# Layer norm statistics staged by ScalarE and GpSimd in pairs of tiles, instead of by VectorE

## The chip, the cores and the metric

The kernel runs on all 8 cores of one Trainium2 chip, one sequence of the batch on each core, with no traffic between them. The metric is the device time in microseconds of the slowest core. A core has five engines with a queue each: TensorE (PE, matmuls), VectorE (DVE), ScalarE (ACT), GpSimd (POOL) and SyncE (SP), which only issues DMAs here. ScalarE and GpSimd issue some of the DMAs too.

## The reference

Two layers on x of shape 8 x 2048 x 1024, in float32. LN is the layer norm without weights.

```python
def _layernorm(x, axis=-1, eps=1e-5):
    m = jnp.mean(x, axis=axis, keepdims=True)
    v = jnp.var(x, axis=axis, keepdims=True)
    return (x - m) / jnp.sqrt(v + eps)

x = x + L0_attn(_layernorm(x))   # minGRU-like scan h; layer norm of h, times gamma, + beta, + its input
x = x + L0_ffn(_layernorm(x))    # 1024 -> 4096 -> 1024, weights fake-quantised to 8 bits, plus LoRA
x = x + L1_attn(_layernorm(x))   # time-mix, k, v, r products, wkv scan, output product
x = x + L1_ffn(_layernorm(x))    # three products of 1024 x 1024, tanh
```

So there are five layer norms: of x before each of the four blocks, and of the scan's result h inside the first. The fake quantisation needs the largest absolute value of each of the two weight matrices.

## The kernel before

**Layout.** Each core holds its sequence transposed: 1024 features are 8 row blocks (`kk` or `m`, 0 to 7) of 128 partitions, and 2048 steps of time are 4 tiles (`n`, 0 to 3) of 512. `X0` and `H0` are 8 blocks of 128x2048 float32 each, `XB0` the same in bf16, `E0` four blocks (`EX[0]` and `EX[1]` hold the rows of a norm), `SC` scratch with the slots `SCR[0]` to `SCR[4]` of 128x512 float32. The eight PSUM banks are `PB0` to `PB7`.

**Queues and waits.** The order of the work on each engine is the order of the source. The helper `body` (line 105) opens a block of instructions for one engine; it waits first for what `k.dep` has gathered and for the engine's own last count, then runs the given function. `mark` counts up the engine's semaphore, `chain` does so and waits for it.

**Statistics of a norm.** The features lie along partitions, so the sums over them are made on TensorE: a 128x128 matrix of ones (`ONESB`) times the tile gives the sum in every partition. `ln_stats` (line 284) goes over the 32 tiles of a tensor in SBUF, `kk` outside and `n` inside. Each tile is staged into one of two slots (`SCR[0]` and `SCR[1]`, each seen as 1024 bf16): the first half takes a bf16 copy, the second the square. Then two matmuls add them into banks `n` and `NT + n` over the eight `kk`. A slot may be filled again when its matmuls are done (`slot_tok`). With `stage="v"`, the default and what all three callers use, VectorE does the copy and the square of one tile in a block. The function also has a branch `stage == "sg"`, which no caller uses before the change.

`_ln_rows` (line 347) then has VectorE scale the sums, form the variance and its reciprocal, and ScalarE take the square root. It is unchanged, as is `ln_stream_stats` (line 379), which does the statistics of the third and fourth norm on tiles loaded from DRAM; the fourth (line 1345) has a `stage="sg"` of its own, with one tile at a time.

**The three callers.** (1) Line 475, norm of x: `X0` is loaded by two DMAs of 4 MB, followed by the small parameters; the weights `WZ` and `WH` are loaded by GpSimd's queue. ScalarE first makes small exponentials of the parameters (`p0s`, `p0d2`). After the rows, VectorE and GpSimd make the normalised `XB0`. (2) Line 683, norm of h. The loop before it (m over 8 blocks, n over 4 tiles) has products on TensorE, sigmoids on ScalarE, combinations and a scan per m on VectorE (`scan_done[m]`). Between them VectorE takes the absolute maximum of the weights, in chunks loaded through `qring` (`Pass1`, line 521). `pass1_fin` (line 645) stands between loop and norm: a GpSimd reduction over the partitions, a memset on VectorE, a broadcast matmul on TensorE (`bcm`) and four small VectorE operations. After the norm h, scaled and added to its inputs, makes `H0` (`comb_done`). (3) Line 759, norm of `H0`. Before it stand a second `pass1_fin` and eight DMAs on ScalarE's queue that spill `H0` to DRAM (`spl`, line 754), the one of block m when `comb_done` of that block is there.

**`Pass1`.** It keeps the token of its last reduction in `self.prev`, None at first, on which the next reduction waits.

Of the kernel before, what the change touches and what calls it, by code (L numbers as in the profile page):

```python
# [181 lines left out]
def build(T=2048, debug=False):  # L182
# [54 lines left out]
    EX = [E0[:, i * RT:i * RT + T] for i in range(4)]  # L237
# [5 lines left out]
    with nc.Block() as blk:  # L243
        k = K(nc, blk)
# [226 lines left out]
        def ln1_tok(kk, n):  # L471
# [1 line left out]

        k.dep(["tensor"], at=tmax(smalls_v))
        ln1_rows = ln_stats(lambda kk, n: Xr[kk][:, n * NSZ:(n + 1) * NSZ],
                            ln1_tok, EX[0], EX[1])
        stats_T = ("tensor", k.snap("tensor"))

        xhat_tok = {}
# [41 lines left out]
        class Pass1:  # L521

            def __init__(self, hbm, nrows, ping, gate=None):
                self.hbm = hbm
                self.ping = ping
                self.chunks = [(kk, c) for kk in range(nrows)
                               for c in range(hbm.shape[1] // QCH)]
                self.ci = 0
                self.prev = None
                def mz(v, ping=ping):  # L530
                    v.memset(MX[:, ping:ping + 1], 0.0)
                    v.mark()
                k.V(mz)

            def emit(self, n):
                end = min(self.ci + n, len(self.chunks))
                while self.ci < end:
                    ci = self.ci
                    kk, c = self.chunks[ci]
                    ping = self.ping  # L540
                    slot, tok = qring.load(
                        ci, self.hbm[kk * 128:(kk + 1) * 128,
                                     c * QCH:(c + 1) * QCH])
                    k.dep(["vector"], at=tmax(tok, self.prev))
                    def red(v, ci=ci, slot=slot, ping=ping):
                        v.tensor_reduce(MX[:, 12:13], slot, AX.X,
                                        OP.max, apply_absolute_value=True)
                        v.chain()
                        v.tensor_max(
                            MX[:, ping + (ci + 1) % 2:ping + 1 + (ci + 1) % 2],  # L550
                            MX[:, ping + ci % 2:ping + 1 + ci % 2],
                            MX[:, 12:13])
                        qring.release(ci, ("vector", v.mark()))
                    k.V(red)
                    self.prev = ("vector", k.snap("vector"))
                    self.ci += 1
# [18 lines left out]
        scan_done = {}  # L575
# [69 lines left out]
        def pass1_fin(fcol, qcol, bank, vtok):  # L645
# [19 lines left out]
            def qsc(v, qcol=qcol, bank=bank):  # L665
# [15 lines left out]
        qfc_tok = pass1_fin(f_fc, 0, 7, f_fc_tok)  # L681

        lnh_rows = ln_stats(lambda kk, n: HD[kk][:, n * NSZ:(n + 1) * NSZ],
                            lambda kk, n: scan_done[kk], EX[0], EX[1])

        xring = Ring(k, [EXf[2][:, i * 512:(i + 1) * 512] for i in range(4)],
                     ["rr0", "rr1", "rr2", "rr3"], issue_eng="sync",
# [1 line left out]
        comb_done = {}  # L689
# [62 lines left out]
        for m in range(8):  # L752
            k.dep(["scalar"], at=comb_m[m])
            def spl(y, m=m):
# [2 lines left out]
            sp2_at[m] = ("sp2w%d" % m, 16)  # L757

        ln2_rows = ln_stats(lambda kk, n: Hr[kk][:, n * NSZ:(n + 1) * NSZ],
                            lambda kk, n: comb_done[(kk, n)], EX[0], EX[1])  # L760
        xh2_tok = {}
        k.dep(["vector", "gpsimd"], at=tmax(ln2_rows))
        def xh2_v(v):
# [778 lines left out]
```

How the kernel before makes its waits and increments, by code:

```python
    def mark(self):  # L47
        K = self._K
        c = K.ch[self._n]
        assert self.last is not None, "mark with no pending instruction"
        self.last.then_inc(c.sem, 1)
        c.val += 1
        self.last = None
        return c.val
# [1 line left out]
    def chain(self):  # L56
        v = self.mark()
        self._e.wait_ge(self._K.ch[self._n].sem, v)
# [1 line left out]
    def wait(self, name, val):  # L60
        if val > 0:
            self._e.wait_ge(self._K.ch[name].sem, val)
# [1 line left out]
    def dma(self, name, out, in_, **kw):  # L64
        K = self._K
        c = K.ch[name]
        ins = self._e.dma_start(out=out, in_=in_, **kw)
        ins.then_inc(c.sem, 16)
        c.val += 16
        self.last = None
        return c.val
# [34 lines left out]
        def run(eng):  # L106
            ctx = Eng(self, eng, name)
            pend = self.pend[name]
            own = self.ch[name]
            if own.val > pend.get(name, 0):
                pend[name] = own.val
            if pend:
                for p, v in sorted(pend.items()):
                    if v > 0:
                        eng.wait_ge(self.ch[p].sem, v)
                pend.clear()
            fn(ctx)
            if ctx.last is not None:
                ctx.mark()
# [149 lines left out]
            def f(g):  # L269
                ins = g.dma_start(out=out, in_=in_, **kw)
                ins.then_inc(c.sem, 16)
                g.last = None
# [1209 lines left out]
        def fin(y):  # L1482
            for name, v in sorted(fin_vals.items()):
                if v > 0:
                    y.wait_ge(k.ch[name].sem, v)
```

## Time and profile before

| | us |
|---|---|
| median of 2 runs | 2946.62 (2943.77 to 2949.47) |
| the profiled execution | 2951.28 |
| its span on the slowest core (core 3) | 2949.7 |
| spans of the 8 cores | 2912.0 to 2949.7 |
| VectorE busy | 1456.2 (49%) |
| TensorE busy, matmuls | 1334.9 (45%) |
| ScalarE busy, of it table loads | 654.4, 309.2 |
| GpSimd busy | 276.1 (9%) |

Busy times are sums over one core's span; an engine may be nearly idle overall and still set the pace of a stage. All times below are from core 3, in microseconds from the start of its span. ACT_TABLE_LOAD is an instruction by which ScalarE loads the tables of its functions; nobody writes it in the source, the compiler places it.

### The profile page before, as it was taken

To read this page: it belongs to the slowest core of one execution; us is meant where nothing else is said; L and a number is where in the kernel's file an instruction comes from. 1 tells how busy PE (TensorE), PEld (TensorE's weight loads), DVE (VectorE), ACT (ScalarE), POOL (GpSimd) and SP (SyncE) were. 2 spreads that over 40 slices of the span, in tenths; PEclk is the share of its full clock that TensorE was granted. 3 is DMA by queue.
4 is the path that set the end of the run, shared out by engine and by line. 5 is a ranking of instruction groups with operands and counts; after the bars stand their busy time and mean duration, and the time that the engine had idled before them with its cause. 6 is when DMAs were issued, how large, how long until landed. Compare 5 with 4: busy or idle time off the path is not lost.

```text
span 2949.7 us, 18381 instructions; the slowest of 8 cores (2912.0 to 2949.7 us)
## 1 busy us (share of the span) xinstructions
PE 1334.9 (45%) x4868; PEld 483.7 (16%) x4868; DVE 1456.2 (49%) x1702; ACT 654.4 (22%) x766; POOL 276.1 (9%) x219
## 2 busy tenths in 40 slices
PE   3144443004044804878888330265055454130986
PEld 0011110000000300333333100122022111000332
DVE  3866667888898996101010136654945411034232
ACT  0023330000287400030313000045034300250003
POOL 0300000230310001000000002400300000222000
PEclk9997776555555955989999755677577767555998
DMA  7223331340033330101010661100100144823006
GB/s 186 86 85 108 107 111 32 78 121 15 17 108 108 101 106 13 43 15 56 2 58 1 120 152 38 43 0 0 38 5 1 22 94 87 153 86 114 1 7 207
DMA packets 73843, 200.95 MB, mean 68 GB/s; under 512 B 9440, under 2 KB 9440, under 8 KB 70928
## 3 DMA queue, kind: packets, MB, share of 16 engines
q1 hardware_dynamic: 59952, 165.76, 19.6%
q0 software_dynamic: 11776, 19.34, 4.5%
q10 hardware_dynamic: 2016, 14.68, 1.3%
q8 instruction: 44, 0.72, 0.1%
q14 instruction: 55, 0.45, 0.1%
HBM read 179.24 MB, written 39.85 MB: 74 GB/s over the span
## 4 chain that ended last, share of the span: by engine, by line
DVE 38%; PE 22%; DMA 18%; ACT 11%; issue 7%; POOL 1%; DVEq 1%; SPq 1%; ACTq 0%; POOLq 0%
PE PB L38 22%; DVE SC L38 10%; DVE X L38 10%; DMA SC<-SP 8%; DVE E L38 7%; ACT L38 5%; DVE AT L38 4%; DVE H L38 3%; DVE XB L38 3%; ACT SC L38 3%; DMA E<-SP 2%; ACT X L38 2%; DMA E<-WPRT 2%; DVE MX L38 2%; DMA AT<-SP 2%
## 5 line engine op out<-in xcount | busy, mean ns | idle before, releaser
L38 ACT ACT_TABLE_LOAD x241 | 309.2, 1283 | 2280.9 <-PE PB L38 974.6
L38 PE MATMUL PB<-XB,X 128*128 128x512 bf16 x1280 | 294.1, 390 | 154.6 <-POOL XB L38 97.5
L38 PE MATMUL PB<-XB,H 128*128 128x512 bf16 x896 | 233.1, 420 | 270.5 <-DVE X L38 162.0
L38 PE MATMUL PB<-E,H 128*128 128x512 bf16 x1152 | 274.5, 403 | 68.8 <-DVE X L38 50.1
L38 PE MATMUL PB<-X,H 128*128 128x512 bf16 x512 | 148.4, 461 | 323.4 <-ACT SC L38 114.9
L38 PE MATMUL PB<-SC,ONESB 128*128 128x512 bf16 x320 | 154.8, 584 | 267.0 <-DVE SC L38 154.9
L38 DVE TENSOR_SCALAR AT<-PB,QS,SMT 128x512 f32<-128x512 f32 x32 | 25.9, 810 | 465.1 <-PE PB L38 337.7
L38 PEld LDWEIGHTS PB<-XB,X 128*128 128x128 bf16 x1280 | 125.1, 100 | 324.0 <-issue 188.9
L38 PEld LDWEIGHTS PB<-XB,H 128*128 128x128 bf16 x896 | 91.0, 106 | 413.1 <-issue 338.1
L38 PEld LDWEIGHTS PB<-E,H 128*128 128x128 bf16 x1152 | 117.3, 103 | 225.9 <-issue 107.0
L38 PE MATMUL PB<-H,X 128*128 128x512 bf16 x512 | 120.8, 397 | 21.1 <-ACT X L38 7.9
L38 PEld LDWEIGHTS PB<-X,H 128*128 128x128 bf16 x512 | 57.4, 114 | 414.8 <-issue 378.5
L38 PE MATMUL PB<-E,ASL 16*128 16x512 bf16 x64 | 37.1, 580 | 174.6 <-ACT E L38 93.7
L38 DVE TENSOR_TENSOR X<-PB,SC 128x512 f32<-128x512 f32 x32 | 22.1, 691 | 182.0 <-DMA SC<-SP 182.0
L38 PE MATMUL PB<-MX,SC 1*128 1x1 f32 x4 | 1.1, 343 | 198.6 <-DVE SC L38 198.6
L38 PE MATMUL PB<-SC,ASL 16*128 16x512 bf16 x64 | 36.5, 570 | 119.9 <-DVE H L38 90.6
L38 ACT ACTIVATE E<-PB,SMT,QS 128x512 bf16<-128x512 f32 x128 | 89.1, 776 | 0.4
L38 DVE CAST H<-PB 128x512 bf16<-128x512 f32 x64 | 39.7, 682 | 98.6 <-PE PB L38 98.6
L38 POOL TENSOR_TENSOR E<-E 128x1024 f32<-128x1024 f32 x28 | 78.1, 2789 | 95.9 <-DMA E<-SP 92.4
L38 PEld LDWEIGHTS PB<-SC,ONESB 128*128 128x128 bf16 x320 | 21.7, 103 | 397.2 <-issue 397.2
L38 DVE TENSOR_SCALAR SC<-E,DRV 128x1024 f32<-128x1024 f32 x16 | 12.1, 753 | 127.0 <-ACT SC L38 127.0
L38 DVE TENSOR_SCALAR E<-PB 128x512 f32<-128x512 f32 x40 | 24.4, 680 | 91.6 <-PE PB L38 91.6
(136 smaller groups left out, 1927.1 us busy)
## 6 DMA issues: line engine op xcount, KB each, us to landing
AT<-WFCT SPq DMA_DIRECT2D x32, 512.0 KB, 3.7
E<-WFCT SPq DMA_DIRECT2D x32, 512.0 KB, 3.9
SC<-WPRT SPq DMA_DIRECT2D x32, 512.0 KB, 3.7
SC<-SP SPq DMA_DIRECT2D x64, 256.0 KB, 3.5
AT<-SP SPq DMA_DIRECT2D x32, 512.0 KB, 3.7
E<-SP SPq DMA_DIRECT2D x32, 512.0 KB, 3.7
E<-SP SPq DMA_DIRECT2D x56, 256.0 KB, 5.1
X<-XT SPq DMA_DIRECT2D x2, 4096.0 KB, 28.9
```

Of the source, the lines that this page charges most:

```text
L38: ins = f(*args, **kw)
```

## The change

`ln_stats` is called with `stage="sg"` in all three places. In that branch the tiles go in pairs. ScalarE makes the two bf16 copies (an activation with the function Copy), GpSimd the two squares (a product of the tile with itself), each in a block of its own. Both blocks wait for the matmuls of both slots and for the tokens of both tiles; TensorE then waits for both engines and does the four matmuls of the pair in one block. The slots and their number, the sums and their order stay.

In `Pass1` the token `self.prev` is set, after the memset that clears the running maximum, to VectorE's count at that point.

```diff
         ln1_rows = ln_stats(lambda kk, n: Xr[kk][:, n * NSZ:(n + 1) * NSZ],
-                            ln1_tok, EX[0], EX[1])
+                            ln1_tok, EX[0], EX[1], stage="sg")
...
                 k.V(mz)
+                self.prev = ("vector", k.snap("vector"))
...
         lnh_rows = ln_stats(lambda kk, n: HD[kk][:, n * NSZ:(n + 1) * NSZ],
-                            lambda kk, n: scan_done[kk], EX[0], EX[1])
+                            lambda kk, n: scan_done[kk], EX[0], EX[1],
+                            stage="sg")
...
         ln2_rows = ln_stats(lambda kk, n: Hr[kk][:, n * NSZ:(n + 1) * NSZ],
-                            lambda kk, n: comb_done[(kk, n)], EX[0], EX[1])
+                            lambda kk, n: comb_done[(kk, n)], EX[0], EX[1],
+                            stage="sg")
```

## Rows read from the trace of the kernel before

**Rows 1.** The page: its header and the chain that ended last, by engine.
```profile
span 2949.7 us, 18381 instructions; the slowest of 8 cores (2912.0 to 2949.7 us)
...
DVE 38%; PE 22%; DMA 18%; ACT 11%; issue 7%; POOL 1%; DVEq 1%; SPq 1%; ACTq 0%; POOLq 0%
```

**Rows 2.** Busy time by stretches: length, engines' busy us and counts, granted clock, DMA.
```profile
42.20:84.40 42.20, 32.38 (x64) 4.38 (x64) 32.91 (x65) 2.75 (x5) 0.00 (x0) 1.00 0.38 70
...
2555.00:2631.00 76.00, 32.38 (x64) 4.37 (x64) 0.00 (x0) 61.20 (x64) 33.22 (x32) 0.50 0.45 130
...
473.50:494.70 21.20, 15.18 (x30) 2.05 (x30) 16.42 (x33) 0.00 (x0) 0.00 (x0) 0.51 0.00 0
494.70:513.60 18.90, 10.06 (x34) 2.18 (x34) 16.43 (x33) 0.00 (x0) 0.00 (x0) 1.00 0.00 1
```

**Rows 3.** Timeline, first norm: start, duration, engine, operation, [idle before <-releaser].
```profile
42.20 0.43 DVE L38 CAST SC<-X 128x512 bf16<-128x512 f32 x1 [0.17 <-DVE DRV L38]
...
43.37 1.01 PE L38 MATMUL PB<-SC,ONESB 128*128 128x512 bf16 x2 [43.37 <-DVE SC L38]
...
44.93 0.21 ACT L38 ACTIVATE DRV<-DRV 128x8 f32<-128x8 f32 x1
...
45.90 0.43 DVE L38 CAST SC<-X 128x512 bf16<-128x512 f32 x1 [0.24 <-PE PB L38]
...
46.24 0.68 DVE L38 TENSOR_TENSOR SC<-X 128x512 bf16<-128x512 f32 x1
...
47.17 1.01 PE L38 MATMUL PB<-SC,ONESB 128*128 128x512 bf16 x2 [0.26 <-PE PB L38]
...
83.15 1.01 PE L38 MATMUL PB<-SC,ONESB 128*128 128x512 bf16 x2 [0.43 <-DVE SC L38]
```

**Rows 4.** Timeline, statistics of the fourth norm.
```profile
2555.62 1.03 POOL L38 TENSOR_TENSOR SC<-AT 128x512 bf16<-128x512 f32 x1 [8.58 <-DMA AT<-SP]
...
2557.92 1.01 PE L38 MATMUL PB<-SC,ONESB 128*128 128x512 bf16 x2 [51.04 <-POOL SC L38]
...
2559.08 1.04 POOL L38 TENSOR_TENSOR SC<-E 128x512 bf16<-128x512 f32 x1 [1.19 <-PE PB L38]
...
2566.66 1.28 ACT L38 ACT_TABLE_LOAD   x1 [3.09 <-DMA AT<-SP]
...
2567.95 0.63 ACT L38 ACTIVATE SC<-AT 128x512 bf16<-128x512 f32 x1
...
2568.83 1.01 PE L38 MATMUL PB<-SC,ONESB 128*128 128x512 bf16 x2 [3.79 <-ACT SC L38]
```

**Rows 5.** Groups of instructions from 2555 to 2631: count | busy, mean ns | idle before.
```profile
L38 ACT ACT_TABLE_LOAD x32 | 41.1, 1283 | 228.7 <-DMA AT<-SP 224.1 <-DMA E<-SP 2.2
```

**Rows 6.** Timeline, ScalarE in the loop after the first norm.
```profile
176.03 0.69 ACT L38 ACTIVATE X<-PB,DRV 128x512 f32<-128x512 f32 x1
176.62 1.26 ACT L38 ACTIVATE E<-PB,SMT 128x512 f32<-128x512 f32 x2
```

**Rows 7.** All instructions on the ones matrix: ns min/median/max, first and last start.
```profile
L38 PE MATMUL PB<-SC,ONESB x320: 376/586/634, 43.4 to 2630.3; 128*128 128x512 bf16 x160
```

**Rows 8.** Timeline: first scan, end of the loop, broadcast, last statistics pair of LNH.
```profile
192.50 4.42 DVE L38 TENSOR_TENSOR_SCAN H<-X 128x2048 f32<-128x2048 f32 x1
...
453.47 1.26 ACT L38 ACTIVATE E<-PB,SMT 128x512 f32<-128x512 f32 x2
...
471.76 0.55 PE L38 MATMUL PB<-MX,SC 1*128 1x1 f32 x2 [42.66 <-DVE SC L38]
...
512.82 0.59 PE L38 MATMUL PB<-SC,ONESB 128*128 128x512 bf16 x2 [0.54 <-DVE SC L38]
```

**Rows 9.** Timeline: last spill of H, last statistics pair of the second norm.
```profile
668.85 0.33 ACTq L67 DMA_DIRECT2D SP<-H  x1
...
712.51 1.01 PE L38 MATMUL PB<-SC,ONESB 128*128 128x512 bf16 x2 [0.26 <-PE PB L38]
```

**Rows 10.** Groups of GpSimd's instructions over the span, shapes kept apart.
```profile
L38 POOL TENSOR_TENSOR XB<-SC,E 128x512 bf16<-128x512 f32 x16 | 24.4, 1524 | 2.3
```

## The prediction

> **What bounds the kernel now.** I read the header and the chain of work that ended last on the page first. The chain goes by VectorE for 38% of the span and by TensorE for 22% [rows 1]: no single engine is full, the kernel is a row of stages that wait for one another. So the three stages that the change touches have to be found in the trace and read one by one. They are the three places where the ones matrix is multiplied with a staged tile: 43 to 84 us (first norm, "LN1"), 474 to 513 us (norm of the scan's result, "LNH") and 671 to 714 us (second norm, "LN2").
>
> In each of them VectorE stages a tile (a cast and a square), TensorE multiplies it, and nothing else runs: in LN1 the stretch holds 32.9 us of VectorE and 32.4 us of TensorE, with ScalarE and GpSimd almost empty [rows 2]. The timeline shows the tempo. VectorE starts a cast at 45.90 and its square ends at 46.92 (46.24 + 0.68); the matmul pair starts 0.25 later, at 47.17, takes 1.01, and the next cast into that slot follows 0.24 behind it. One slot's circle is 1.02 + 0.25 + 1.01 + 0.24 = 2.52 us, and there are two slots, so a tile costs 1.26 us [rows 3]. From the first pair at 43.37 to the last at 83.15 are 31 tiles: 1.28 us each. In all three stages the normalised values wait for the last matmul, so what a stage grows by goes straight to the end of the kernel. No work stands behind the statistics on VectorE that could be drawn forward: the next thing in its queue is the rows, which read the finished sums.
>
> **The change, part by part.** All three calls take the branch "sg", which no stage of this program takes through `ln_stats` now. It removes 32 casts and 32 squares per stage from VectorE and puts the casts on ScalarE and the squares on GpSimd. It also moves from tiles to pairs of tiles: both engines wait until both slots are free, fill both, and TensorE then makes four matmuls. With two slots and pairs of two, the slots are no longer filled while the others are multiplied. So the circle of a pair must be added up end to end. The nearest work is the last norm (LN4, 2555 to 2631 us), which already stages with ScalarE and GpSimd, though from a loaded tile and with one tile at a time.
>
> 1. *Release of the slot.* TensorE's pair ends at 2558.93 (2557.92 + 1.01), GpSimd starts at 2559.08: 0.15 us. I take it for ScalarE too [rows 4].
> 2. *ScalarE.* Each block of instructions of LN4 begins with a table load: 32 loads in 32 blocks, 1283 ns each [rows 5], and the load comes after the wait, not beneath it: at 2566.66 it starts when the DMA is there, and the copy follows at 2567.95, 1.29 later [rows 4]. The copy takes 0.63. Here a block has two copies with no wait between them. In the loop after LN1 two such activations of 0.69 start 0.59 apart (176.03 and 176.62), so they overlap by 0.10 [rows 6]; two copies thus take 0.53 + 0.63 = 1.16. ScalarE: 1.29 + 1.16 = 2.45.
> 3. *GpSimd, in parallel.* A square takes 1.03 to 1.04 [rows 4]. Two take 2.08 if they touch; a gap as wide as 0.20 between them would make it 2.28. Either is under ScalarE's 2.45, so I cost GpSimd at nothing: the table load covers it, by 0.17 to 0.37 us.
> 4. *Hand-over to TensorE.* The copy ends at 2568.58, the matmul starts at 2568.83: 0.25 [rows 4].
> 5. *Four matmuls.* A pair takes 1.01 and a single one has a median of 0.586 [rows 3, 7], so each further one adds 0.42: 1.01 + 0.85 = 1.86.
>
> The circle: 0.15 + 2.45 + 0.25 + 1.86 = 4.71 us per pair, against 2.52 for two tiles now. The new one is nearly twice as long, because casts and squares, though parallel now, have got the table load in front and the matmuls behind them.
>
> Then each stage's start and end, with 15 circles after the first pair (15 x 4.71 = 70.7):
> - LN1. ScalarE still has the small exponentials to do and is free at 45.14 (44.93 + 0.21), where VectorE began at 42.20 [rows 3]. Table load and copies from 45.21 end at 47.66, matmuls 47.91 to 49.77, last ones end at 120.4. Now they end at 84.16: **+36.3**.
> - LNH. ScalarE's last evacuation before it ends at 454.7 [rows 8], so the first pair lies ready. TensorE must first take the broadcast of the maximum, which waits for VectorE's memset behind its last reductions and ends at 472.31 (471.76 + 0.55) [rows 8]. First four matmuls to 474.3, last to 544.9, against 513.41: **+31.5**.
> - LN2. ScalarE's queue holds the eight spills of H first; the last one is issued at 668.85 and done at 669.18 [rows 9]. So load and copies run to 671.7, matmuls to 673.8, the last to 744.5, against 713.52: **+30.9**.
>
> Sum: +98.7 us. What VectorE is spared (35 us per stage) is worth nothing, as it only waits for the same sums.
>
> The granted clock of TensorE: LNH began at 0.51 and rose to 1.00 near 494.7 us, and there the pair fell from 1.01 to 0.59 us; TensorE had been busy 15.2 of the 21.2 us before [rows 2]. LN2 and LN4 never show the fast pairs. LN4 has TensorE busy 32.4 of 76 us at 0.50 (the level of 1.2 GHz), and the new stages would have 1.86 of 4.71, much the same share. So I count every matmul slow, LNH's second half too, whose loss is in the +31.5.
>
> The other edit sets `self.prev` to VectorE's own count after the memset. `body` waits for the engine's own last count in any case, and that count is never lower; the instructions stay the same. Cost nothing; there is nothing that it could hide.
>
> A rule of the Trainium skill speaks against step 2. "ScalarE: Activation LUTs", section "Table sets: the hidden batching unit", has copy in every set as filler, and says that functions of one set need one load between them; by it the pairs would need no loads and the circle would be GpSimd's. This case's trace does not agree for this program: 32 loads for 32 blocks of copies alone. Against step 3 stands "GPSIMD Engine Reference", section "Elementwise — side-by-side cycle accounting", with a two-input operation about twice as long as on VectorE. That would be an estimate of 1.37 us for a square, and +13 us or so in the sum; the trace has 1.04.
>
> **The rivals.**
> - *GpSimd sets the circle.* The 16 products of GpSimd after LN1 take 1.52 us each [rows 10], with VectorE at work beside most of them. If the squares take that long, GpSimd needs 3.04, 0.59 over ScalarE's 2.45: 45 x 0.59 = +27 more, 3072 us. For it: no square from X or H was ever made by GpSimd. Against it: LN4's squares are the same operation and shape with VectorE idle, as it will be here.
> - *No table load in the circle* (absent or beneath the wait). GpSimd then leads with 2.08: 45 x 0.37 = 17 less, and 1.3 each off LN1 and LN2: 3026 us. Against it are all 32 loads of LN4 [rows 5]. By the skill's rule on table sets the time would come out here.
> - *TensorE at the fast level.* The four matmuls then take 1.01 (0.59 for the first two, and 2 x 0.21, as the shortest single one is 0.376 [rows 7]): 48 x 0.85 = 41 less, 3004 us. LNH has shown the fast level; but after a stretch with a busy share nearly twice that of the new circle.
> - *The other side: the statistics run ahead.* They no longer need VectorE, and the scans' tiles come one by one, the first from 192.5 us [rows 8]. If ScalarE, GpSimd and TensorE took them as they come, only the last two pairs of LNH would be left, and it would be over at about 473 instead of 513.4 us; LN2 likewise, some 9 us after 669 instead of 45. Sum: 36 - 40 - 35 = -39 us, 2908 us, not slower. The point that decides is TensorE's queue: the broadcast of the maximum stands before the first statistics matmul and needs VectorE's last reduction (it starts at 471.76 [rows 8]), and at LN2 the spills stand before the copies. With only two slots nothing past the first pair can go ahead. Queues keep their order, so this falls.
>
> **How the numbers follow.** The profiled execution took 2951.28 us (span 2949.7); with 98.7 that is 3050.0. The median of the runs is 4.7 us lower, 2946.62, so the forecast is 3045.3 us, 3.3% slower. Chances: the forecast with its small errors 0.82; GpSimd sets the circle 0.08; no table load 0.04; TensorE fast 0.03; statistics ahead 0.02; something unseen 0.01. The range runs from the case without the load to that with GpSimd's slow squares, 3026 to 3072. That takes in the unknown widths too: no overlap of the copies is +4.5 us, GpSimd's gap nothing. All cases but the last two end over 2% slower (2946.6 x 1.02 = 3005.6; the case of the fast matmuls lies right at that line and I split it). Two per cent is about what a measurement of this kernel can tell from no change. Slower 0.95, within 2% 0.04, faster 0.01.
>
> **What would show it.** In the changed profile: in the three stages GpSimd squares and ScalarE copies of 128x512 from X and H, with a table load before each pair of copies, 48 more loads in all (289); matmuls of the ones matrix in fours of 1.86 us, whose starts lie 4.7 us apart; ScalarE's copy as what released TensorE; the rows on VectorE starting near 120.6 us instead of 84.3, then everything about 36 us late, 68 us after LNH and 99 us after LN2, and the same from there to the end. The step on GpSimd is wrong if TensorE waits for GpSimd in these stages; the step on the level if fours take 1.0 us; the step on the queues if the first fours of LNH come before 471 us. The whole forecast is wrong if one of the stages ends within 45 us, since then pairs overlap in a way I rule out, or if a later stage gives time back, for which I see no slack: what follows each norm waits for its rows.

## The result and the profile after

The changed kernel takes 3049.83 us (median of 11 runs), the kernel before 2947.43 us (10 runs beside it). The ratio is 1.0341, with a 95% interval of 1.0319 to 1.0364: 3.4% slower. The forecast was 3045.3 us, 3.3% slower. In some executions of any of these kernels the cores of one half of the chip show a lower clock and take some per cent longer; every ratio here is formed without them, and of the first measurement with four slots too few were left for a ratio.

The page of the changed kernel, header and busy times:

```profile
span 3040.3 us, 18446 instructions; the slowest of 8 cores (3016.0 to 3040.3 us)
...
PE 1334.9 (44%) x4868; PEld 491.3 (16%) x4868; DVE 1362.7 (45%) x1510; ACT 771.2 (25%) x910; POOL 371.7 (12%) x315
```

TensorE does the same work in the same busy time. VectorE has lost 93 us of work (1456.2 before), and the kernel is 102 us longer. What VectorE gave up has gone to ScalarE (+117 us) and GpSimd (+96 us), and more than half of ScalarE's share is table loads: 289 of them now, 241 before.

The timeline of the changed kernel at the start of the first norm, the counterpart of [rows 3] (start, duration, engine, operation, [idle before <-what ended it]):

```profile
46.96 1.28 ACT L38 ACT_TABLE_LOAD   x1
48.25 1.15 ACT L38 ACTIVATE SC<-X 128x512 bf16<-128x512 f32 x2
...
49.65 1.86 PE L38 MATMUL PB<-SC,ONESB 128*128 128x512 bf16 x4 [49.65 <-ACT SC L38]
...
51.65 1.28 ACT L38 ACT_TABLE_LOAD   x1 [2.25 <-PE PB L38]
51.72 2.04 POOL L38 TENSOR_TENSOR SC<-X 128x512 bf16<-128x512 f32 x2 [27.91 <-PE PB L38]
52.94 1.15 ACT L38 ACTIVATE SC<-X 128x512 bf16<-128x512 f32 x2
...
54.34 1.86 PE L38 MATMUL PB<-SC,ONESB 128*128 128x512 bf16 x4 [2.83 <-ACT SC L38]
...
120.36 1.86 PE L38 MATMUL PB<-SC,ONESB 128*128 128x512 bf16 x4 [2.83 <-ACT SC L38]
```

This is one turn of the circle, read from release to release. TensorE's four matmuls end at 51.51 (49.65 + 1.86). ScalarE's table load starts at 51.65 and its two copies end at 54.09. GpSimd starts at 51.72 and is done at 53.76. TensorE starts at 54.34, released by ScalarE ("ACT SC"), after 2.83 us of idleness. From the first four at 49.65 to the sixteenth at 120.36 are 15 turns: 4.71 us each. Nothing in this list overlaps but copy and square.

The stretches of the three norms in the changed kernel (length, then busy us and counts of TensorE, its weight loads, VectorE, ScalarE and GpSimd, the granted clock, DMA):

```profile
49.60:122.30 72.70, 29.83 (x64) 6.91 (x64) 0.00 (x0) 36.48 (x45) 30.52 (x30) 1.00 0.13 22
509.30:581.90 72.60, 29.83 (x64) 6.93 (x64) 0.49 (x4) 36.48 (x45) 30.52 (x30) 0.50 0.00 0
742.00:814.60 72.60, 29.83 (x64) 6.90 (x64) 0.00 (x0) 36.48 (x45) 30.52 (x30) 0.50 0.00 0
```

Three equal stretches of 72.6 us, where [rows 2] and the timeline of before had 38.5 to 41. VectorE does nothing at all in two of them. TensorE's 29.8, ScalarE's 36.5 and GpSimd's 30.5 us are each well under 72.6: no engine is full, their times add up.

Which core is the slowest differs from execution to execution, so I compared where the last statistics matmul ends on each of the 8 cores in the two profiled executions. These are means over the cores:

| end of | before | after | later by | forecast |
|---|---|---|---|---|
| first norm | 84.8 | 121.6 | 36.8 | 36.3 |
| norm of the scan | 512.9 | 579.0 | 66.1 | 67.8 |
| second norm | 713.2 | 811.5 | 98.4 | 98.7 |
| the span | 2930.2 | 3029.3 | 99.1 | 98.7 |

The loss arises in the three norms and nothing behind them gives any back. The slowest cores alone differ by 90.6 us (2949.7 and 3040.3): the cores of one execution lie up to 38 us apart, and most of that spread arises after the second norm, in both kernels.

### The profile page after: what moved, and what is told of

It is laid out like the page before. It is cut to its first block, busy times and chain, and to the rows that moved or that the text cites. A ratio compares the mean times of both kernels' runs of the same rounds, so it can differ in the third digit from the quotient of the medians.

```text
span 3040.3 us, 18446 instructions; the slowest of 8 cores (3016.0 to 3040.3 us)
## 1 busy us (share of the span) xinstructions
PE 1334.9 (44%) x4868; PEld 491.3 (16%) x4868; DVE 1362.7 (45%) x1510; ACT 771.2 (25%) x910; POOL 371.7 (12%) x315
## 4 chain that ended last, share of the span: by engine, by line
DVE 35%; PE 23%; DMA 17%; ACT 14%; issue 7%; POOL 1%; DVEq 1%; SPq 1%; ACTq 0%; POOLq 0%
PE PB L38 23%; DVE X L38 9%; DVE SC L38 8%; DMA SC<-SP 7%; DVE E L38 7%; ACT L38 6%; ACT SC L38 4%; DVE AT L38 4%; DVE H L38 3%; DVE XB L38 3%; DMA AT<-SP 3%; ACT X L38 2%; DMA E<-WPRT 2%; DVE MX L38 2%; DMA SMT<-SM 1%
## 5 line engine op out<-in xcount | busy, mean ns | idle before, releaser
L38 PE MATMUL PB<-E,H 128*128 128x512 bf16 x1152 | 278.4, 407 | 66.1 <-DVE X L38 47.6
L38 PEld LDWEIGHTS PB<-XB,H 128*128 128x128 bf16 x896 | 90.6, 105 | 409.1 <-issue 333.0
L38 PEld LDWEIGHTS PB<-SC,ONESB 128*128 128x128 bf16 x320 | 29.5, 117 | 480.1 <-issue 480.1
L38 PE MATMUL PB<-SC,ASL 16*128 16x512 bf16 x64 | 36.3, 566 | 119.7 <-DVE H L38 93.5
L38 DVE CAST H<-PB 128x512 bf16<-128x512 f32 x64 | 39.7, 682 | 98.4 <-PE PB L38 98.4
```

What stands on the lines that cost most here:

```text
L38: ins = f(*args, **kw)
```

## The experiments

Two ways to explain 4.71 us per pair were to be told apart. By the theory, the circle is long because filling and multiplying stand end to end, and the table load is one of the pieces on it. By its rivals, the load is the real cost, or GpSimd sets the pace, or ScalarE and GpSimd are just slow at the work. All edits are to the changed kernel unless something else is said. A pair's turn in the kernel before is 2.52 us.

**One norm alone.** The kernel before, with the new staging in the first norm only.

```diff
-                            ln1_tok, EX[0], EX[1])
+                            ln1_tok, EX[0], EX[1], stage="sg")
```

> The kernel before with stage="sg" in the first norm alone, and self.prev as before. Theory (each norm is a chain of its own that sets the end, so the costs add up): the first norm's last statistics matmul ends 36 us later and everything behind it shifts by that much, 2947 + 36 = 2983 us. Rival (a later stage gives time back, for instance through transfers that have landed by then, or the cost lies in one of the other two norms): less than 2970 us.

Measured: 1.0133 of the kernel before (1.0089 to 1.0177), which at 2947 us is +39 us (26 to 52), with 36 expected. The first norm's matmuls take 72.6 us here, as in the changed kernel, and on the mean over the cores they end 36.3 us later and the span 34.3 us later than in the kernel before (121.1 and 2964.5, against 84.8 and 2930.2). So the cost of a norm passes to the end nearly whole, and with the table above the three add up. In this execution the scan's norm took 41.1 us in VectorE's way on the slowest core, all with slow matmuls:

```profile
550.61 1.01 PE L38 MATMUL PB<-SC,ONESB 128*128 128x512 bf16 x2 [0.26 <-PE PB L38]
...
551.88 1.01 PE L38 MATMUL PB<-SC,ONESB 128*128 128x512 bf16 x2 [0.25 <-PE PB L38]
```

The fast second half that [rows 8] show for the kernel before, with pairs of 0.59 us, is thus no fixed part of it: here core 0 had it (37.4 us for the norm) and most others did not. In the profiled execution of the kernel before, the norm took 38.5 us on core 3, and 39.9 to 41.3 on the other cores.

**Four slots.** The slots `SCR[0]` to `SCR[3]`, so that a pair is filled while the one before is multiplied, with a wait before the first use of the two new ones (not shown here); nothing else.

```diff
-                    at = tmax(slot_tok[0], slot_tok[1],
+                    at = tmax(slot_tok[p0 % 4], slot_tok[(p0 + 1) % 4],
...
-                            sb = bc16(SCR[(p0 + j) % 2])
+                            sb = bc16(SCR[(p0 + j) % 4])
```

> The changed kernel with four staging slots (SCR 0 to 3) instead of two, so that a pair can be filled while the pair before it is multiplied. Theory (the cost is that filling and multiplying stand end to end): the pair's period falls from 4.71 us to ScalarE's own 1.29 + 1.15 + about 0.13 = 2.57 us, 45 x 2.14 = 96 us less, about 2954 us. Rival (ScalarE and GpSimd are slower at the work by themselves, whatever the slots): the period stays above 4 us and the time above 3020 us.

> The kernel with four slots once more, beside the one above: its period was 2.63 us, so 45 x 2.08 = 94 us less than 3050 are expected, 2956 us, some 0.4% over the kernel before and 15 us over four slots with one load.

Measured: 2961.73 us in the first profiled execution; the ratio is that of the second measurement of the same kernel: 1.0069 (1.0044 to 1.0095). Of the 3.4% four slots give back 2.7. The timeline of the first:

```profile
62.00 1.28 ACT L38 ACT_TABLE_LOAD   x1 [0.19 <-ACT SC L38]
...
62.07 1.87 PE L38 MATMUL PB<-SC,ONESB 128*128 128x512 bf16 x4 [0.76 <-ACT SC L38]
...
63.30 1.15 ACT L38 ACTIVATE SC<-X 128x512 bf16<-128x512 f32 x2
64.14 2.04 POOL L38 TENSOR_TENSOR SC<-X 128x512 bf16<-128x512 f32 x2 [0.60 <-PE PB L38]
...
64.69 1.87 PE L38 MATMUL PB<-SC,ONESB 128*128 128x512 bf16 x4 [0.76 <-ACT SC L38]
```

The matmuls start at 62.07 and 64.69, 2.62 us apart instead of 4.71. ScalarE now works while TensorE multiplies, and its own turn sets the pace: 1.29 load, 1.15 copies and 0.19 in which it waits for its own last copy at the border of the block. The same engines with the same instructions and the same loads take 41.6 us for the first norm, in both measurements, where the changed kernel took 72.6. So the loads and the slower engines cost little once they overlap with the matmuls; that they stood in line with them is what cost. Some 4 to 5 us of what is left arise before the staging: on the mean over the cores the first norm's matmuls start at 48.6 us (49.5 in the second measurement) against 44.2 in the kernel before, as ScalarE has its parameter work first.

**One tile per block**, two slots.

```diff
-                for p0 in range(0, len(tiles), 2):
-                    pair = tiles[p0:p0 + 2]
-                    at = tmax(slot_tok[0], slot_tok[1],
+                for p0 in range(0, len(tiles)):
+                    pair = tiles[p0:p0 + 1]
+                    at = tmax(slot_tok[p0 % 2],
```

> The changed kernel with one tile in a block of each engine instead of two, two slots as before. Theory: a slot's circle of 0.15 + 1.29 + 0.63 + 0.25 + 1.01 = 3.33 us is now shorter than two turns of ScalarE, which needs a table load for every tile: 2.05 us per tile as in the fourth norm, 4.1 per two tiles, 45 x 0.61 = 27 us less than 3050, about 3022 us. If the table load cost nothing, GpSimd's or the slot's circle would give 1.7 us per tile, 2990 us or less. If blocks are dear by themselves, it would be slower than 3050.

Measured: 1.0256 (1.0203 to 1.0309), which is 3023 us at 2947, with 3022 expected.

```profile
59.33 1.28 ACT L38 ACT_TABLE_LOAD   x1 [0.19 <-ACT SC L38]
...
60.62 0.63 ACT L38 ACTIVATE SC<-X 128x512 bf16<-128x512 f32 x1
61.44 1.28 ACT L38 ACT_TABLE_LOAD   x1 [0.19 <-ACT SC L38]
```

ScalarE's turn is 2.11 us per tile (59.33 to 61.44), with a load for every tile, and TensorE overlaps it. For two tiles that is 4.22 us with two loads, against 4.71 with one load and the matmuls behind it. With twice as many table loads in the three norms (48 more in all, 337) the kernel is faster than the changed one, so the number of loads alone does not explain the time: it matters what they overlap with.

**A third square.** GpSimd makes one square more per pair, after a wait for the first two.

```diff
+                        g.chain()
+                        g.tensor_mul(sb[:, 512:1024], src(kk, n),
+                                     src(kk, n))
                         g.mark()
```

> The changed kernel with one more square in each of GpSimd's blocks: it waits for the first two and writes the second one's result again. It measures how far GpSimd is from setting the pace. Theory (ScalarE's copies come last, GpSimd 0.33 us before): GpSimd's block grows by 1.04 and a gap of 0.1 to 0.2, of which 0.33 is covered, 45 x 0.85 = 38 us more, about 3088 us. Rival (GpSimd sets the pace already): 45 x 1.15 = 52 us more, 3102 us.

Measured: 1.0492 (1.0435 to 1.0548), or 3092 us at 2947.

```profile
61.39 3.22 POOL L38 TENSOR_TENSOR SC<-X 128x512 bf16<-128x512 f32 x3 [2.43 <-PE PB L38]
...
64.97 1.86 PE L38 MATMUL PB<-SC,ONESB 128*128 128x512 bf16 x4 [3.78 <-POOL SC L38]
```

GpSimd's block ends at 64.61 and TensorE starts 0.36 behind it, at 64.97; the next four start at 70.61, a turn of 5.64 us. The block grew by 1.18 us (2.04 to 3.22) and the turn by 0.93, so 0.25 us of GpSimd's time had been covered. That is somewhat less than the 0.33 by which the squares ended ahead of the copies, since TensorE follows GpSimd after 0.36 us and ScalarE after 0.25. The rival by which GpSimd sets the pace already would have given 1.18 per turn. The time at the end can't tell the two apart, as its interval (3076 to 3109 us) holds both 3088 and 3102; the turn in the trace does.

**One table load per norm.** All 32 copies stand in one ScalarE block, with the waits for TensorE inside it; two slots.

```diff
+                def csts(s):
+                    for p0 in range(0, len(tiles), 2):
+                        pair = tiles[p0:p0 + 2]
+                        if p0 >= 2:
+                            s.wait("tensor", t0 + p0 - 0)
...
+                        for j, (kk, n) in enumerate(pair):
+                            sb = bc16(SCR[(p0 + j) % 2])
+                            s.activation(sb[:, 0:512], src(kk, n), AF.Copy)
+                        s.mark()
+                k.S(csts)
```

> The changed kernel with all 32 copies of a norm in one ScalarE block, with the waits for TensorE between the pairs inside it; two slots, GpSimd and TensorE as in the changed kernel. It takes away 15 of 16 table loads per norm and the waits at block borders. Theory (the load of 1.29 us stands in the circle, and GpSimd lies 0.33 us behind it): the circle becomes GpSimd's, 0.21 + 2.04 + 0.25 + 1.86 = 4.36 us, TensorE waits for GpSimd, 45 x 0.34 = 15 us less than 3050, about 3035 us. Rival (the load is the real cost of the change): 45 x 1.29 = 58 us less, 2992 us.

Measured: 1.0335 (1.0308 to 1.0362), not told from the changed kernel's 1.0341. The trace has 45 loads less (244), and:

```profile
60.50 1.15 ACT L38 ACTIVATE SC<-X 128x512 bf16<-128x512 f32 x2 [3.32 <-PE PB L38]
60.55 2.03 POOL L38 TENSOR_TENSOR SC<-X 128x512 bf16<-128x512 f32 x2 [2.43 <-PE PB L38]
...
62.94 1.87 PE L38 MATMUL PB<-SC,ONESB 128*128 128x512 bf16 x4 [2.60 <-POOL SC L38]
...
67.41 1.87 PE L38 MATMUL PB<-SC,ONESB 128*128 128x512 bf16 x4 [2.60 <-POOL SC L38]
```

The copies are done at 61.65 now, but the squares end at 62.58 and TensorE starts at 62.94: the wait has passed from ScalarE to GpSimd, and the turn is 4.47 us. A norm takes 69.0 us, 3.5 less, 10.5 for the three. I expected 15 and had the hand-over from GpSimd too short (0.25 where it is 0.36). The two ratios have intervals of some 7 us to each side, so they cannot show 10 us; the profiled executions do, where on the mean over the cores the second norm ends 9.4 us earlier than in the changed kernel (802.1 against 811.5) and the span 9.9 us earlier. The rival that the load is the real cost (58 us, 2992 us) falls: that would be a ratio of 1.015.

**Four slots and one load together.** Both edits above.

> Four slots and one ScalarE block per norm together. Theory: with nothing end to end the pace is that of the slowest engine, GpSimd with 2.04 us per pair and about 0.2 between blocks, 2.25 us, just under the 2.52 us of VectorE's way before: 45 x 2.46 = 111 us less than 3050, about 2940 us, within one per cent of the kernel before. If GpSimd or ScalarE slow each other or TensorE when they all run at once, the period is over 2.6 us and the time no better than with four slots alone.

Measured: 0.9979 (0.9961 to 0.9997), 2941 us at 2947. Now GpSimd sets the pace, with nothing but 0.27 us between its blocks:

```profile
59.12 2.04 POOL L38 TENSOR_TENSOR SC<-X 128x512 bf16<-128x512 f32 x2 [0.27 <-POOL SC L38]
...
61.42 2.04 POOL L38 TENSOR_TENSOR SC<-X 128x512 bf16<-128x512 f32 x2 [0.27 <-POOL SC L38]
```

Its turn is 2.30 us, 2.25 expected; the norms take 36 to 37 us on that core, 35 to 38 on all. Some of TensorE's fours took 1.02 us here instead of 1.86 and nothing came of it, since GpSimd sets the pace. So even with the slots and the load out of the way, ScalarE and GpSimd as stagers are hardly better than VectorE alone was with two slots.

**Another split.** The kernel before, where ScalarE copies, VectorE squares and TensorE multiplies, each in one block per norm, with four slots and waits tile by tile. In `pre` an engine waits for TensorE's matmuls of the tile four before, which had the slot, and for the source tile. GpSimd is left out.

```diff
+                def cps(s):
+                    for i, (kk, n) in enumerate(tiles):
+                        pre(s, i, kk, n)
+                        s.activation(bc16(SCR[i % 4])[:, 0:512], src(kk, n),
+                                     AF.Copy)
+                        s.mark()
+                k.S(cps)
+                def sqs(v):
+                    for i, (kk, n) in enumerate(tiles):
+                        pre(v, i, kk, n)
+                        v.tensor_mul(bc16(SCR[i % 4])[:, 512:1024],
+                                     src(kk, n), src(kk, n))
+                        v.mark()
+                k.V(sqs)
```

> The kernel before with the work split otherwise: ScalarE makes the copies and VectorE the squares, each in one block per norm, TensorE's matmuls in one block, four slots, a wait for each tile. Theory: per tile TensorE needs 0.85 us at its slow level, VectorE 0.68 + 0.1, ScalarE 0.53, so 32 tiles take 27 us instead of 41. First norm: ScalarE starts about 4 us later, 9 us gained; norm of the scan 12, second norm 14 us gained: 35 us less than 2947, about 2912 us (1.2% faster). If the waits inside the block cost as much as block borders, the tile stays at 1.1 us or more and the gain is under 15 us.

Measured: 0.9828 (0.9793 to 0.9864), 1.7% faster than the kernel before (1.4 to 2.1%) and the fastest of all; 1.2% was expected. The stretches of the three norms:

```profile
50.40:69.80 19.40, 19.02 (x64) 6.47 (x64) 17.22 (x28) 17.22 (x31) 0.00 (x0) 1.00 0.51 86
454.30:475.40 21.10, 19.62 (x64) 6.50 (x64) 19.92 (x35) 17.02 (x30) 0.00 (x0) 0.87 0.00 1
632.50:652.50 20.00, 19.64 (x64) 6.57 (x64) 19.33 (x32) 17.45 (x31) 0.00 (x0) 0.88 0.04 17
```

The norms take 19 to 21 us where I had expected 27, and three engines are busy for nearly all of it. I had counted every matmul at the slow level. In the last two the granted clock is 0.87 and 0.88 instead of 0.50, between the levels of 1.2 and 2.4 GHz because part of the stretch ran at each: in the scan's norm it is 0.51 up to 460 us and 1.00 from there on. In the first norm TensorE had multiplied without a pause since 50.49 us when, at 53.8, the starts of its matmuls went from 0.427 to 0.216 us apart. The timeline has TensorE's last 47 matmuls of the first norm in 13.99 us, 0.60 for a tile's two, with VectorE at the same pace:

```profile
55.87 13.32 DVE L38 TENSOR_TENSOR SC<-X 128x512 bf16<-128x512 f32 x22
...
55.73 13.99 PE L38 MATMUL PB<-SC,ONESB 128*128 128x512 bf16 x47
```

So VectorE's squares set the pace at 0.605 us each. They follow each other faster than the 0.68 + 0.1 that I had taken from blocks with a border each.

This kernel changes three things at once: the split, the number of slots and the blocks. No run has VectorE alone with four slots, so what each is worth is not shown. An estimate for the slots: in the fast half of the scan's norm before, VectorE does not wait for TensorE, and a tile takes 0.59 + 0.54 = 1.13 us [rows 8], which is 36 us for 32 tiles. By that, more slots without a split would save some 5 us of the 41, and the rest of the 21 would be the split, the joined blocks and the faster matmuls.

**The edit to `self.prev`** was not run by itself. By the source it changes nothing: the only block that it could delay is VectorE's own next reduction, and `body` makes every block wait for its engine's own last count already.

## Why the prediction was right

Point by point, by its own steps.

- *The circle.* Forecast 4.71, measured 4.71. Release of ScalarE 0.14 (0.15 forecast), load and copies 2.44 (2.45), hand-over 0.25 (0.25), four matmuls 1.86 (1.86). The overlap of two copies by 0.10, taken from another activation in the loop [rows 6], came out as 0.11 (2 x 0.63 - 1.15). The terms lay ready in the trace of before because another norm already did the same work there [rows 4]; what had to be added was only the order.
- *GpSimd covered.* The two squares take 2.04 us, release 0.21, and before its statistics matmuls (of all five norms) TensorE waits 78 times for ScalarE and once for GpSimd. The cover of 0.17 to 0.37 us was measured at 0.25 by the third square. The rival of slow squares fell: 1.04 and 1.05 us each from X and H, not 1.52. It had a true core, though. GpSimd squares the first pair of the second norm ahead of time, beside VectorE's last products, and there both engines are slow:

```profile
708.92 2.70 POOL L38 TENSOR_TENSOR SC<-H 128x512 bf16<-128x512 f32 x2 [0.21 <-POOL MX L38]
709.39 1.34 DVE L38 TENSOR_TENSOR H<-SC,X 128x512 f32<-128x512 f32 x1
```

  The two squares took 1.26 and 1.48 us instead of 1.04, and VectorE's product 1.34, where the last one of its kind took 0.69 in the kernel before (668.08 us), with GpSimd not at work beside it. Beside one of VectorE's reductions (first pair of the scan's norm, 472.05 us) they took 1.04 as ever. So the forecast held also because VectorE has no such products to do during the statistics.
- *The load on the path.* 289 loads, as forecast. "ScalarE activation tables: per-element evaluation and per-set limits" of the Trainium skill says, in "Table sets in the compiler and the runtime", that the back end places the loads per block. The traces agree: 48 more blocks, 48 more loads, and 45 less with one block per norm in place of 16. The rule of the Trainium skill on table sets, which the prediction weighed, came true in these traces within a block and not across blocks: 32 copies of one function shared one load once they stood in one block.
- *The stages.* +36.8, +66.1 and +98.4 us against 36.3, 67.8 and 98.7. The first norm starts with ScalarE's parameter work, as forecast: the load for its first copies starts 3.5 us after the first one for that parameter work (46.96 and 43.44). At the scan's norm the first four matmuls start at 509.34, right behind the broadcast that ends at 508.98, and ScalarE's copies for them are done by 494.1. At the second norm the load starts at 739.14, behind the last spill:

```profile
738.67 0.33 ACTq L67 DMA_DIRECT2D SP<-H  x1
...
739.14 1.28 ACT L38 ACT_TABLE_LOAD   x1 [125.78 <-DVE SC L38]
```

  Of the 31.5 us for the scan's norm some 2.6 were core 3's fast half, which most other cores did not have; on the mean over cores the step is 29.3 (66.1 - 36.8), and the second norm's is 32.3 against 30.9. So the mechanism is right and each stage within 2.2 us, but that the sum agrees to 0.4 us is luck: one stage was forecast too long and the other two too short.
- *TensorE's level.* All the new stages ran slow: 0.50 granted in two of them, every group of four 1.86 us. The first norm shows 1.00 and yet the same 1.86 us, as it did before with pairs of 1.01 [rows 2, 3]; at that point the durations say more than the column. The rival of the fast level fell in the changed kernel, but in the last experiment the fast level came, and with VectorE's shorter turn it was worth some 7 us per norm. I had left it out of that expectation.
- *The statistics run ahead.* They did not. In the changed kernel TensorE waits 42.66 us before the broadcast, as before [rows 8].
- *The other edit.* Nothing in the result points to it, and no run has it alone.
- *Nothing given back.* The shift at the end is 99.1 us on the mean over the cores, 98.4 at the last of the three norms. VectorE waits longer in front of each norm's rows:

```profile
DVE E L38 <- PE PB L38: 311.4, 5, 85.5
```

  Five waits with 311 us in total, 91.6 before; the longest, 85.5, is not in these three norms and was there before (86.1). What was taken from VectorE's work, 31 us per norm (the prediction says 35), came back as its waiting, and more than that.

## What to carry to other kernels

Before moving work to idle engines, add up the circle of one buffer: release, fill, hand-over, use. With no more buffers than one turn fills, every term of it is paid in full, and of two engines that fill in parallel the slower one counts. Give a turn its own second set of buffers before judging the engines: here that alone took the cost from 3.4% to 0.7%. And keep a run of activations in one block, with the waits inside, since each block of them pays a table load of 1.28 us, after its wait.

## What the runs showed of the hardware that I had not expected

- In one block with waits between them, VectorE's squares of 128x512 follow each other every 0.605 us, although each is recorded with 0.68. In blocks of their own a cast and a square took 1.02 plus the border.
- TensorE follows GpSimd later than ScalarE: 0.36 against 0.25 us from the end of the recorded instruction to the first matmul.
- At a block's border ScalarE waits 0.19 us and GpSimd 0.27 us for its own last result before it starts (with four slots; once in the first norm ScalarE waited 0.49, for a reason not shown).
- In the last experiment TensorE was busy for 19.0 to 19.6 of 19.4 to 21.1 us of each norm, and a tile's two matmuls came every 0.60 us where they had taken 1.01. With VectorE's squares at 0.605 that gave about 7 us a norm on top of the 14 expected from the overlap. TensorE was still not full there: a matmul is recorded with 0.377 us, but a tile's two start 0.215 us apart, and VectorE set the pace.
- GpSimd's square of 128x512 took 1.48 us in place of 1.04, and VectorE's product 1.34 in place of 0.69, where the two engines worked at the same time; beside a reduction on VectorE the square took 1.04.
